# Frequency mixing: six of twelve matrix loads moved from the first transform step (ScalarE's queue) to the start of the mixing (SyncE's queue)

## The reference, cut to what matters

```python
Vf = jnp.fft.rfft(phi, n=n, axis=0)
Uf_p = jnp.fft.rfft(u, n=n, axis=1)
Uf_m = jnp.fft.rfft(u * sgn3, n=n, axis=1)
U_plus = jnp.fft.irfft(Vf[None, :, :, None] * Uf_p[:, :, None, :], n=n, axis=1)[:, :sl]
U_minus = jnp.fft.irfft(Vf[None, :, :, None] * Uf_m[:, :, None, :], n=n, axis=1)[:, :sl]
...
out = jnp.einsum('btkd,k,kde->bte', U_plus, s, Mpp)
out = out + jnp.einsum('btkd,k,kde->bte', U_minus, s, Mpm)
```

## Time and profile before

| | us |
|---|---|
| median of 3 executions | 2806.27 |
| lowest, highest | 2798.83, 2819.66 |
| profiled execution, its own time | 2806.48 |
| its span in the profile | 2804.7 |
| `forward`, from its first instruction to the start of the next stage's | 575.35 to about 761 |
| first matmul of `spectrum` (L909) | 768.99 |
| first matmul of the mixing (L924) | 781.17 |
| last matmul of the mixing (L924) | 1977.2 |

### The profile page before, as it was taken

How to read it: one execution, slowest core, us unless ns; L and a number is a source line. 1 busy time by engine, 2 the same in 40 slices (tenths; PEclk the granted TensorE clock), 3 DMA queues, 4 the chain that set the end, 5 groups by cost and what they waited for, 6 DMA issues and landing times. The chain is left out here.

```text
span 2804.7 us, 78734 instructions
## 1 busy us (share of the span) xinstructions
PE 2373.1 (85%) x34528; PEld 1806.6 (64%) x34528; DVE 1495.6 (53%) x3482; ACT 1307.3 (47%) x2623; POOL 360.5 (13%) x639
## 2 busy tenths in 40 slices
PE   3457999856599999999999999999795984899898
PEld 2237888823288888888888888888433741344444
DVE  3852333446346655665665566566211552676777
ACT  3453333344266566665665565565210563333332
POOL 1311111123300000000000000000111001122221
PEclk7677877978799999999999999999996886899999
DMA  6457444457611111111111111110498410000000
GB/s 191 148 140 175 84 90 85 96 174 220 211 43 46 45 43 40 45 46 46 46 45 46 31 29 44 46 23 22 154 301 277 132 48 13 13 20 25 21 24 27
DMA packets 154975, 235.08 MB, mean 84 GB/s; under 512 B 18058, under 2 KB 112371, under 8 KB 151120
## 3 DMA queue, kind: packets, MB, share of 16 engines
q1 hardware_dynamic: 122392, 134.74, 16.6%
q0 software_dynamic: 31920, 88.25, 11.4%
q10 hardware_dynamic: 324, 7.08, 1.1%
HBM read 141.68 MB, written 88.31 MB: 82 GB/s over the span
## 5 line engine op out<-in xcount | busy, mean ns | idle before, releaser
L1027 DVE COPY spc_g<-spc_pz 128x512 f32<-128x512 f32 x1024 | 629.4, 683 | 310.5 <-PE spc_pz L924 310.5
L997 ACT ACTIVATE spc_g<-spc_pz 128x512 f32<-128x512 f32 x1024 | 549.2, 610 | 286.3 <-PE spc_pz L924 286.0
L924 PE MATMUL spc_pz<-spc_v,mats_as 108*128 108x128 bf16 x8192 | 553.7, 219 | 15.3 <-issue 2.7
L924 PEld LDWEIGHTS spc_pz<-spc_v,mats_as 108*128 108x128 bf16 x8192 | 473.7, 97 | 104.2 <-ACT spc_g L997 32.2
L945 PE MATMUL spc_pz<-spc_g,spc_u 128*20 128x128 f32 x16384 | 471.0, 274 | 23.4 <-DVE spc_g L1027 17.4
L945 PEld LDWEIGHTS spc_pz<-spc_g,spc_u 128*20 128x20 f32 x16384 | 451.6, 134 | 51.2 <-ACT spc_g L997 30.2
L1542 PE MATMUL moe_ex<-moe_ew,moe_d 128*128 128x512 f32 x512 | 250.6, 612 | 32.9 <-DVE moe_yt L1699 32.5
L1699 DVE SCALAR_TENSOR_TENSOR moe_yt<-moe_ex,moe_gb,moe_yt 128x128 f32<-128x128 f32 x768 | 209.6, 344 | 102.1 <-ACT moe_yt L1601 96.9
L566 DVE SCALAR_TENSOR_TENSOR inv_xo<-inv_pa,inv_mask,inv_xo 128x256 f32<-128x256 f32 x256 | 123.6, 484 | 228.5 <-PE inv_pa L524 195.7
L544 ACT ACTIVATE inv_b<-inv_pb 112x1024 f32<-112x1024 f32 x128 | 125.9, 1022 | 225.6 <-PE inv_pb L503 225.6
L909 PE MATMUL spc_pu<-spc_f,spc_s 128*128 128x256 f32 x768 | 207.2, 395 | 22.0 <-DMA spc_s<-s_sf 22.0
(11 more groups left out here) (217 smaller groups left out, 2287.5 us busy)
## 6 DMA issues: line engine op xcount, KB each, us to landing
s_yd<-spc_yo SPq DMA_DIRECT2D x128, 160.0 KB
s_sf<-fwd_so SPq DMA_DIRECT2D x16, 1024.0 KB, 10.2
spc_s<-s_sf POOLq DMA_DIRECT2D x32, 512.0 KB, 5.9
ivs_y<-s_yd POOLq DMA_DIRECT2D x32, 512.0 KB, 5.6
s_td<-ivs_to SPq DMA_DIRECT2D x32, 512.0 KB, 5.1
ln_t<-s_td SPq DMA_DIRECT2D x32, 512.0 KB, 3.8
lnc_xc<-in_x SPq DMA_DIRECT2D x32, 256.0 KB, 5.4
s_xn<-lnc_xn SPq DMA_DIRECT2D x64, 128.0 KB
```

The source lines that it names most:

```text
L924: m = pe.matmul(pz[:, (p + 2) % 3, e // 4, 2 * FT * (e % 4):2 * FT * (e % 4) + 2 * FT], AS[:, x, 8 * p + e, :], V[:, k, x, :, FT * t:FT * ...
L997: act.activation(g_out(p, 0), g_in(p, 0), ACT.Copy).then_inc(ga, 1)
L1027: v.tensor_copy(g_out(p, 1), g_in(p, 1)).then_inc(gd, 1)
```

## The change

The first transform step loads only the six groups of the first sign, one per pass, after the second quarter. The six groups of the second sign are loaded by SyncE's queue at the very start of `spectrum`'s block. TensorE waits for them once, before the first use of the second sign (f = 0, t = 0, x = 1). The bytes loaded and everything computed stay the same.

```diff
@@ forward, ScalarE
             def mixers(i):
-                g, x = divmod(i, 2)
-                act.dma_start(AS[KX * g:KX * g + KX, x].rearrange("k e d -> k (e d)"),
-                              S["AS"][x, A_PARTS[g]].rearrange("k e d -> k (e d)")).then_inc(as_in, 16)
+                act.dma_start(AS[KX * i:KX * i + KX, 0].rearrange("k e d -> k (e d)"),
+                              S["AS"][0, A_PARTS[i]].rearrange("k e d -> k (e d)")).then_inc(as_in, 16)
...
-                    if 1 <= n < 7 and c % 2:
-                        mixers(2 * n - 2 + c // 2)
+                    if 1 <= n < 7 and c == 1:
+                        mixers(n - 1)
...
-            act.wait_ge(as_in, 16 * 12)
+            act.wait_ge(as_in, 16 * 6)
@@ spectrum
+        as_in = A.sem("as_in")
...
                 for t in range(NTL):
                     for x in range(2):
+                        if f == 0 and t == 0 and x == 1:
+                            pe.wait_ge(as_in, 16 * 6)
                         make_g(f, k, t, x, last)
                         make_y(f, k, t, x)
...
         @block.sync
         def _(sp):
+            for g, part in enumerate(A_PARTS):
+                sp.dma_start(AS[KX * g:KX * g + KX, 1].rearrange("k e d -> k (e d)"),
+                             S["AS"][1, part].rearrange("k e d -> k (e d)")).then_inc(as_in, 16)
```

## The result

20 timings of each kernel: 2818.44 us median with the change (2788.0 to 2838.75), 2794.7 before (2763.42 to 2835.04). The ratio is 1.0074, 95% interval 1.0048 to 1.0101: about 21 us slower, a loss clear of noise, but (save for the last hundredth of a percent of the interval) inside the 1% that the prediction called no change. The ratio leaves out executions more than 1.5% above the fastest of their kernel, three of the change and by that rule six of before, where a single execution took only 2763.42; the means of all 20 differ by 16 us. The predicted 2807 and its range (2794 to 2822) hold the time, but in part by luck: both terms of the sum were too small and of opposite sign, and the kernel before turned out 12 us faster in 20 timings than in the three that the forecast started from.

A forecast was written before the change was run, and what follows sets the result against it. The prediction took TensorE, busy 85% of the span, as the main load, with first-step stalls for `fw` behind shared DMA engines. It summed 2806.5 - 9 (first step) + 10 (mixing's start) = 2807 us, range 2794 to 2822.

The forecast's parts named there:

- The new wait: First use of the second sign in the mixing: matrices land before it, so the wait costs nothing; cover 13 us.
- Gain of the first step: 9 us: First transform step: six loads fewer shorten stalls for `fw`; 9 us, ends 2 and 16.
- the forecast 20 to 26: First transform step: waits for `fw` of about 20 to 26 us in the changed profile instead of 33.1.
- The cap of 4.2 us per removed load: First transform step: each removed load gives back at most 4.2 us, and no more than the next `fw` stall.
- Loss at the start: 10 us: Mixing's start: SyncE's six loads delay the tokens and so TensorE; +10 us, between 5 and 17.
- the first frequency's tokens come after three turns of matrices: Mixing's start, nine loaded engines: queues alternate by whole shares of a transfer, delaying first tokens 9.3 us.
- 1.55 us per 32 KB, the rate of the tokens themselves: Mixing's start: assumed time of one 32 KB matrix packet on an engine, taken from the tokens' transfer.
- a gap over 26 us: Mixing's start: GpSimd's first issue to first L909 matmul, 7.6 us before, about 17 forecast; over 26 speaks for rival 2.
- rival 2: Mixing's start: tokens stand behind all six loads, 12 packets, 19 to 26 us; total 2823 us; chance 0.13.
- Rival 1: Start hides the loads and the first step's gain is nearly whole: -14 + 4 us, total 2796; chance 0.17.
- rival 3: Mixing's second sign: slow loads, over 3.3 us per packet, make its matmuls wait; total 2825 us; chance 0.03.
- The forecast's own case, three turns of matrices: First step gains 9 us, mixing's start loses 10 as tokens wait three turns; total 2807 us; chance 0.67.

The follow-up runs named there:

- the late version: Against the change: SyncE's six second-sign loads wait until the second frequency's tokens have landed; gap 7.9 us, ratio to before 0.9955.
- the second profile: The change run again unaltered: first step 169.8 us, gap from GpSimd's first issue to first L909 matmul 35.6 us, ratio to before 1.0032.
- The kernel before in pieces: Against before: all twelve loads stay in the first step, each slot issuing four pieces of 18 rows by 8 KB; first step 182.3 us, ratio 0.9949.
- three loads first: Against the change: three of SyncE's six loads go at once, three wait for the second frequency's tokens; gap 20.8 us.
- 4 KB pieces: Against the change: the six loads cut into 48 of 18 rows by 4 KB, group by group, same place; gap 14.3 us.

## Why the prediction was right, and where not

**Sign and bound.** A gain in the first step and a loss at the start that nearly cancel, inside 1%: right. That 2818.44 lies in the range is partly luck: the range was laid around 2806.5, reaching 15 us above it, and in the timing itself the change is 16 to 24 us slower than before, by whichever average. The rest of the program unchanged, no wait at the second sign (834.34 above), the second frequency's tokens in time (12.3 us from L909 to L924, expected 13): right. The new wait was covered with room: the six loads took 33 us in the late version, and before the change the second sign began 39 us after GpSimd's first issue, so loads issued at once would be in even without the late start. Issued 13 us later, as in the late version, they are not. That all six loads use the same nine engines is borne out: with the seven others done, the DMA share was 0.62 from 788 to 797 us and 0.42 from 797 to 802, 8.8 of 16 engines on average.

**Gain of the first step: 9 us, measured 18** (16 to 18 in the two profiles of the change, 14.5 to 19.6 in the other kernels with the same step). The cause was right, and the waits for `fw` (20.8 us, 20.7 in the second profile) fell into the forecast 20 to 26. Two things were missed. The cap of 4.2 us per removed load does not hold: the stall of 11.3 us lost 8.1 with one load fewer ahead of it. And the sum counted these waits alone, while a third of the gain lay elsewhere: 3.8 us (2.4 in the second profile) in shorter matmuls, which ran slower after long waits (eight of L689 took 3.60 us after the wait of 11.3 and 1.90 where there was none), and 2 mostly in waits for ScalarE. The table of stretches gives the right size directly: the stage moves 210 GB/s over its 186.01 us before and 212 over 167.94 after, with a DMA share of 0.65 in both. It goes at the pace of its transfers, and 3.54 MB at 211 GB/s are 16.8 us. By this reading, an argument from one stage, a stall for one table was only where the pace became visible. The kernel before in pieces supports it: with the same bytes in another shape only 3.7 us came.

**Loss at the start: 10 us, measured 28.** Two terms were mis-sized. First, "the first frequency's tokens come after three turns of matrices", six large packets: they met all twelve. In the earlier trace rows GpSimd's packets looked like waiting for whole shares of a transfer; three loads first (20.8), 4 KB pieces (14.3) and the packet counts show instead that, on a loaded engine, about one packet of each queue is served in turn. An engine has 24 token packets of 4 KB and 12 of 32 KB, so the tokens end after all the matrices. In the change's stretch from 788 to 797 us, 35 large packets stand beside 0.18 MB, 44 token packets. The earlier trace rows had left out SyncE's row for 617 to 617.9 us,

```profile
q1 hardware_dynamic: 60, 0.36, 97.0%
```

so GpSimd's 32 packets were not served between two stores but beside SyncE's. Why GpSimd had none in the next 2 us no run told. The Trainium skill, "DMA: Bandwidth & Descriptors", section "Queues, rings and completion order", has an engine drain a packet of typically 9 to 17 descriptors before it switches; by that turns would be larger than these runs show, and the measurement decides. Second, "1.55 us per 32 KB, the rate of the tokens themselves": a large packet took 2.2 to 2.4. The rows of the matrices themselves had said 2.0 to 2.14; the tokens go to 128 rows and were the wrong neighbour. 12 x 2.3 = 28.

**Rivals.** The prediction's own sign, a gap over 26 us, pointed to rival 2. That rival had the number of packets and nearly the price (19 to 26 us) for another reason, SyncE's loads worked down first, and the packet counts speak against that reason. It had got a chance of 0.13. Rival 1 and rival 3 did not come about. The forecast's own case, three turns of matrices, had got 0.67, too much for a step read from three windows.

## What to carry to other kernels

A load moved to the start of a stage competes with the transfers that the stage cannot start without. Let its issuer wait until those have landed: here one semaphore wait turned +28 us into 0, for 7 us at the second sign. Where two queues share the engines, few large packets beside many small ones win by bytes; cut the ones that can wait to the size of the urgent ones (the gap fell from 35.6 to 14.3 us, the slower issuing included). And if a stage moves the same GB/s with and without a transfer, size the transfer by bytes over that rate, not by the stalls around it (16.8 us here, where 14.5 to 19.6 were measured).

## What the hardware showed unexpectedly

- 18 neighbouring rows of 32 KB load at an estimated 129 to 135 GB/s, by nine engines or by sixteen (2.2 or 4.1 us a packet), while tokens for 128 rows ran at 1.5 us per 32 KB on all sixteen.
- A narrow load slows its neighbours beyond the engines it sits on. Beside it, the tokens in the change took 45.0% of 20 us x 16 engines for 1.64 MB, 144 us of engine time, against 79 us for 1.69 MB alone. The matrices' 53.7% are 8.6 engines, so the tokens' time lies mostly on the seven without matrices. Why they were slower there was not tested.

```profile
q1 hardware_dynamic: 99, 2.36, 53.7%
q0 software_dynamic: 609, 1.64, 45.0%
```

(The rows are of the change, 767 to 787 us.)
